# Products into unread columns at the heads of three attentions, and 128-row score products in the last attention, of a two-layer decoder

## The reference

```
x = x + L0_attn(ln(x))            # 16 gated heads, 4 causal heads, 4 meta heads, mixed
x = x + L0_xattn(ln(x), ctx)      # cross attention
x = x + L0_ffn(ln(x))             # 8 experts, 2 chosen, and 2 shared; GELU
x = x + L1_attn(ln(x))            # attention on fake-quantised (8 bit) q, k, v
x = x + L1_xattn(ln(x), ctx)      # cross attention, 16 heads of 8 dimensions
x = x + L1_ffn(ln(x))             # 16 experts, 2 chosen, and a shared one; SiLU
```

```
q = (x @ Wq + bq).reshape(B, N, 16, 8)
k = (y @ Wk + bk).reshape(B, M, 16, 8)
v = (y @ Wv + bv).reshape(B, M, 16, 8)
attn = softmax(einsum('bnhd,bmhd->bhnm', q, k) / sqrt(8))
out = einsum('bhnm,bmhd->bnhd', attn, v)
```

## Time and profile before

| what | value |
|---|---|
| median of 3 runs | 769.51 us (767.5 to 772.55) |
| profiled execution | 776.76 us |
| its span, first to last instruction | 775.0 us |
| PE busy | 638.4 us (82%) |
| DVE busy | 419.2 us (54%) |
| ACT busy | 374.7 us (48%) |
| POOL busy | 97.2 us (13%) |
| mean granted clock of PE over the span | 0.830 |

### The profile page before, as it was taken

One profiled execution on the slowest core, in us unless ns is written; L12 is line 12 of the kernel. 1 busy time (PEld: TensorE's weight loads), 2 busy tenths in 40 slices (PEclk: granted clock), 3 DMA queues, 4 the chain that ended last, 5 costly groups with the idle time before them and its releaser, 6 DMA issues. The chain is left out here.

```text
span 775.0 us, 9266 instructions
## 1 busy us (share of the span) xinstructions
PE 638.4 (82%) x3271; PEld 329.1 (42%) x3271; DVE 419.2 (54%) x824; ACT 374.7 (48%) x649; POOL 97.2 (13%) x78
## 2 busy tenths in 40 slices
PE   3389899899996965999999973888888389985798
PEld 1122223223343334898999941122221233333586
DVE  7377775776326645512222358878970754214555
ACT  2157776666650523554444512577876135533331
POOL 7211100100010002600000003960000000003000
PEclk9669999999995756799999966689995655557899
DMA  4342201550023054000000000000000020000000
GB/s 140 81 66 32 69 2 26 68 74 1 2 40 43 0 202 175 1 1 5 10 1 1 1 1 0 1 2 2 2 2 1 1 83 3 3 1 0 1 1 27
DMA packets 14017, 22.68 MB, mean 29 GB/s; under 512 B 2916, under 2 KB 9044, under 8 KB 13588
## 3 DMA queue, kind: packets, MB, share of 16 engines
q1 hardware_dynamic: 12436, 20.78, 11.7%
q10 hardware_dynamic: 1536, 1.31, 0.6%
HBM read 9.99 MB, written 0.52 MB: 14 GB/s over the span
## 5 line engine op out<-in xcount | busy, mean ns | idle before, releaser
L509 DVE TENSOR_REDUCE negmax<-ps 128x2 f32<-128x1024 f32 x96 | 113.8, 1216 | 37.9 <-PE ps L438 37.5
L556 ACT ACTIVATE probs<-ps 128x512 f32<-128x512 f32 x192 | 105.9, 596 | 41.5 <-PE ps L459 40.7
L556 ACT ACTIVATE probs_q<-ps,score_scale 128x512 f32<-128x512 f32 x128 | 78.2, 685 | 16.6 <-PE ps L459 15.5
L1671 PEld LDWEIGHTS ps<-wproj,hid 128*128 128x128 f32 x640 | 83.1, 191 | 6.5
L1671 PE MATMUL ps<-wproj,hid 128*128 128x128 f32 x640 | 83.8, 274 | 0.0
L1724 ACT ACTIVATE hid<-ps 128x512 f32<-128x512 f32 x80 | 47.6, 598 | 66.9 <-PE ps L818 66.9
L818 PE MATMUL ps<-h,wfc 128*128 128x512 f32 x240 | 76.5, 430 | 0.0
L509 DVE TENSOR_REDUCE negmax_q<-ps 128x2 f32<-128x1024 f32 x64 | 73.9, 1205 | 3.9 <-PE ps L438 3.9
L1832 DVE SCALAR_TENSOR_TENSOR x_tok<-ps,comb,x_tok 128x128 f32<-128x128 f32 x64 | 18.0, 344 | 69.6 <-PE ps L1671 69.6
L473 PE MATMUL ps<-probs_q,v_q 128*32 128x512 f32 x256 | 46.8, 730 | 0.0
L438 PE MATMUL ps<-k_gated,q_gated 64*128 64x512 bf16 x128 | 29.8, 427 | 20.1 <-DMA q_gated<-parts 9.3
(11 more groups left out here) (358 smaller groups left out, 931.9 us busy)
## 6 DMA issues: line engine op xcount, KB each, us to landing
q_wide<-parts SPq DMA_DIRECT2D x12, 256.0 KB, 5.7
k_wide<-parts SPq DMA_DIRECT2D x12, 256.0 KB, 7.1
wfc<-in_L_ffn_Wfc_dram SPq DMA_DIRECT2D x1, 2560.0 KB, 9.3
wproj<-in_L_ffn_Wproj_dram SPq DMA_DIRECT2D x1, 2560.0 KB, 15.1
k_gated<-parts SPq DMA_DIRECT2D x9, 128.0 KB, 2.4
q_gated<-parts SPq DMA_DIRECT2D x9, 128.0 KB, 2.4
w<-in_L_ffn_W_dram SPq DMA_DIRECT2D x1, 1024.0 KB, 17.0
square_weights<-in_squares_dram SPq DMA_DIRECT2D x1, 768.0 KB, 7.1
```

The costliest lines, as they stand in the source:

```text
L509: nc.vector.tensor_reduce(maxima, scores, AX.X, ALU.max, negate=True).then_inc(self.a_max_done, 1)
L556: nc.scalar.activation(self.probs[0:size, g % self.P_SLOTS, :], ps[0:size, self.B_BANK + g % self.B_SLOTS, :], ACT.Exp, scale=scale).then_ ...
L1671: last = nc.tensor.matmul(K.ps[:, y_bank(g), i * P:(i + 1) * P], hid[:, m % SLOTS, i * P:(i + 1) * P], wproj[:, FT * e + f, :], start=(f = ...
```

## The change

The change has four edits.

1. `CrossJob.q_at` and `k_at` give all 128 rows. A score product B of the last attention so multiplies all four heads' queries with the block-diagonal keys of one head. The zeros drop out, the result is the same.
2. `keep_busy(K, bank, count)` is new: count products of two weight tiles (128 rows, 128 x 128, float32) into the last 128 columns of a bank, where nothing reads them. `_keep_busy` puts such steps ("K") into the order ahead of every block A up to the first V: `first` of them ahead of the first A, into the given bank, and `each` ahead of the others, into bank 7. The three attentions have (16, 2), (12, 1) and (6, 2).
3. In the quantised attention `within=1` adds one such product to each of the 64 blocks A, behind its wait for the slot and into its own bank, before A writes over it.
4. Two waits for bank 7: the first attention waits for the second of DVE's gate sums, and the first job of the quantised attention for both halves of v scaled by ACT.

```diff
 class CrossJob
     def q_at(self, j, t0, n, more):
-        return self.q[32 * j:32 * j + 32, self.heads[0] // 4, t0:t0 + n]
+        return self.q[:, self.heads[0] // 4, t0:t0 + n]
     def k_at(self, j, t0, n, more):
-        return self.k[32 * j:32 * j + 32, self.heads[0] // 4, j, t0:t0 + n]
+        return self.k[:, self.heads[0] // 4, j, t0:t0 + n]
 class Attention
+    def _keep_busy(self, first, each, bank):
+        head = next(n for n, step in enumerate(self.order) if step[0] == "V")
+        order, count = [], first
+        for step in self.order[:head]:
+            if step[0] == "A":
+                order += [("K", count, bank)] if count else []
+                count, bank = each, self.O_BANK
+            order.append(step)
+        self.order = order + self.order[head:]
     def tensor(self, pe):
         for step in self.order:
             kind, u, i = step
+            if kind == "K":
+                keep_busy(K, i, u)
+                continue
...
                 self.slot_free(pe, step)
+                keep_busy(K, self.bank_of[step], self.within)
                 for half in range(2):
...
+def keep_busy(K, bank, count):
+    for _ in range(count):
+        K.nc.tensor.matmul(K.ps[:, bank, 3 * P:4 * P], K.squares[:, 0, :], K.squares[:, 1, :], start=True, stop=True,
+                           skip_group_check=True)
 GatedAttention
+                         busy=(16, 2, 7))
 gated_attention, tensor
             ln.wait_half(pe, 0)
+            pe.wait_ge(gate_sum, 2)
             att.tensor(pe)
 quantised_attention
-    jobs[0].after = [(n["first_strip"], 2), (n["q_scaled"], 2)]
+    jobs[0].after = [(n["first_strip"], 2), (n["q_scaled"], 2), (n["v_scaled"], 2)]
...
+                         busy=(12, 1, 1), within=1)
 cross_attention_heads
-    att = Attention(K, "attx", jobs, 4, 6, *attention_buffers(sb, "x", st))
+    att = Attention(K, "attx", jobs, 4, 6, *attention_buffers(sb, "x", st), busy=(6, 2, 7))
```

More of the change, by code:

```diff
@@ L278, with __init__ @@
     A_BANK, B_BANK, O_BANK = 0, 4, 7
-    def __init__(self, K, tag, jobs, lead, lead_blocks, probs, osb, negmax, prologue=(), extras=None, held=(), evacuate_on_vector=False):
-        self.evacuate_on_vector = evacuate_on_vector
+    def __init__(self, K, tag, jobs, lead, lead_blocks, probs, osb, negmax, prologue=(), extras=None, held=(), evacuate_on_vector=False,
+                 busy=(0, 0, 7), within=0):
+        self.evacuate_on_vector, self.within = evacuate_on_vector, within
         self.K, self.jobs, self.lead, self.lead_blocks = K, jobs, lead, lead_blocks
@@ L316, in __init__ @@
         self._schedule(extras or {}, held)
+        self._keep_busy(*busy)
         self.free_at, self.count, self.bank_of, uses = {}, {}, {}, []
@@ L893, in decoder_kernel @@
         modulation = sb("modulation", [16, D + 1])
+        K.squares = squares_sb
         for i, n in enumerate(SQUARES):
@@ L976, in __init__ @@
         self.bias_added = K.sem("bias_added")
-        super().__init__(K, "att0", jobs, lead, 8, *bufs[:3], prologue=prologue, extras=extras, held=held)
+        super().__init__(K, "att0", jobs, lead, 8, *bufs[:3], prologue=prologue, extras=extras, held=held,
+                         busy=(16, 2, 7))
         self.mixes = [s for s in self.order if s[0] in "CD"]
@@ L1996, in quantised_attention @@
         jobs[5 * b].after_v = [(n["v_ready"], b + 1)]
-    att = QuantAttention(K, "attq", jobs, 2, 8, *attention_buffers(sb, "q", st), evacuate_on_vector=True)
+    att = QuantAttention(K, "attq", jobs, 2, 8, *attention_buffers(sb, "q", st), evacuate_on_vector=True,
+                         busy=(12, 1, 1), within=1)
     def strip_of(ops, which, g, b):
```

## The result

| | before | changed |
|---|---|---|
| median | 768.81 us (7 runs, 767.5 to 772.55) | 760.58 us (7 runs, 756.01 to 766.0) |
| ratio | | 0.9891, 95% interval 0.9855 to 0.9928 |
| profiled execution, its span | 776.76, 775.0 us | 766.0, 764.2 us |
| PE busy, mean granted clock | 638.4 us, 0.830 | 651.2 us, 0.897 |

The account below looks back on a forecast made before the run. The last attention was taken as bound by PE at half clock. Gains of 17 (last), 1 (first), 0 (quantised head) and 1 (quantised middle) sum to 19 us: median 769.51 to 750.5 us, range 741 to 763.

Parts of the forecast that it names:

- Quantised attention, middle: Between its V: added products lose 3 us (0 to 14), clock returns 4; net 1 us gained, bounds 5 gained, 10 lost.
- the 4 us for the clock: Middle of the quantised attention: clock held at 1.00 instead of 0.92 gives back up to 5.5 us, 4 taken.
- Quantised head: Start of the quantised attention: first A 1.5 us late (1.1 to 2.3), 1.7 back by the first V; net 0.
- The tail: Quantised attention, V after the last A: no added products there, so it keeps its half clock.
- Last attention: B on 128 rows and added products raise the clock: group 7.44 to 4.6 us, 17 us gained, bounds 8 and 21.
- rows in use matter: PE in the last attention, saturated at half clock: rows in use, not busy time alone, seem to decide the clock.
- The price of B on 128 rows: Last attention: paired B run one behind the other, costing 0.21 us per group at full clock, 0.43 at half.
- First attention: Its 38 added products: 1.4 us lost on late blocks, 2.4 gained by earlier clock; net 1 gained, bounds 4 gained, 2 lost.
- The rival "slower": Quantised attention: products ahead of the 64 blocks A become its bound, at half clock 32 us over 26 pairs; 783 us, chance 0.05.

Follow-up runs that it names:

- the 32-column kernel: Changed kernel, with the product ahead of each of the 64 blocks A of the quantised attention cut from 128 to 32 columns; 791.66 us.

## Why the prediction was right or wrong, point by point

The forecast was 750.5 us and the measured time 760.58: sign right, inside the range given (741 to 763), size wrong by 10 us (8.2 gained where 19 were forecast). Of the terms:

- **The step that failed: "Quantised attention, middle".** It found "up to 3.0 us in the worst case" from V to V and 14 us over 26 pairs, and then: "most would fall into idle time; I take 3", less 4 for the clock, net 1 gained. Measured: 3.01 and 3.22 us where 2.48 us lay between two V, 14.03 against 12.14 us a period, and 10.4 us between the medians of the kernels with and without the 64 products. The worst case was right, and the choice inside 0 to 14 failed. By the shown windows PE is busy about 10.1 us of a period without the products (60.06 of 72) and 13.6 with them (82.82 of 85.3). So of 3.5 us of added PE time only 1.6 fell into idle time and 1.9 made the period longer. In the stretches shown, two products of 0.42 less the one wait of 0.30 make 0.54, and the distance grew by 0.53. The busy shares (69.3 of 82 us) couldn't tell this: the longer waits of PE, 1.00 ahead of T and 0.84 ahead of an A, stand in the other distances. The product was also priced by its time in a row of its like, 0.27 us; among 32-row products it holds PE 0.42 us, and the A that had begun beside a B waits for both. Of the 4 us for the clock little was the products' to give. The middle of the kernel before has four dips of 3.4 us, which made a distance 1.1 to 1.3 us longer each, but the same order has none in five other profiles and one in two.
- **Quantised head**: first A forecast 1.5 us late after the spread, measured 1.9 (1.7 in absolute time); the first V 1.3 late instead of level. The tail stayed at half clock in the profiled execution, as said.
- **Last attention**: mechanism right, size low. 4.33 us a group (4.6 forecast), the last groups 3.57, 3.1 twice and 2.36; 21.2 us instead of 17, and 20.9 as medians of the kernel with this part alone. The reason given, that rows in use matter, is half of it: B on 128 rows brings the clock up, but with the 24 products at the head B of 32 rows keep it up too. So the gain would have come by either edit, and the forecast didn't tell them apart.
- **The price of B on 128 rows** (0.21 us a group) didn't show: 4.33 with 128 rows, 4.43 with 32. By the speed-up that the Trainium skill gives for four 32-row products (TensorE: Matmul & The Clock Gate, Part 3, packing small matmuls) it was 7 us in all, an estimate; the trace disagrees for the last attention, where B of 32 rows mostly stood alone anyway. For the quantised one its rule agrees with the trace: products of different strips run at once, and what comes between them takes that away.
- **First attention**: 1 us gained was forecast with bounds of 4 and -2; the kernel with these products alone is 1.2 us faster, within an interval that holds zero.
- **The rival "slower"** had 0.05 with "at full clock 3.0 is the worst I find" against it. Its condition, the half clock, is what two experiments ran into (medians 792.8 and 791.7 us). Why it stayed out of the changed kernel wasn't argued, and the runs don't show it: in that the low chance was luck.

As shifts between the two profiled executions: +10.7 us at the first A of the last attention, -21.2 in that attention, -2.1 in the next products behind it (at full clock now), and +1.9 that a later block gives back. The sum is -10.7, and the two differ by 10.8 (776.76 to 766.0).

## What to carry to other kernels

An added instruction on an engine with idle time is free only as far as waits of that engine shrink by it: look for the waits row by row, between the place where it goes in and the next instruction that another engine waits for, and not at the busy share. Take the worst case where no such wait is found. On TensorE look also at what ran side by side there: a full product between two products of different row strips costs more than its columns. And when two edits lift the same clock, try each alone: here B on 128 rows without any added product gives 750.7 us, where all four edits gave 760.6.

## What was not expected of the hardware

- The granted clock depends on what went before: the same order of work in the last attention ran at 0.50 with PE busy 22.3 of 22.3 us and, after products of 128 rows at its head, at 1.00 with PE busy 12.93 of 13.3 (the kernel with the 24 products alone). The Trainium skill (same page, Part 1, the HAM clock gate) has sustained activity bring up the full clock; 59.6 of 59.6 us busy at 0.50 (the 64 products alone) show that a PE without a gap is not enough here.
- A 128x128 product between 32-row ones holds PE for 0.42 us, a second one right behind it only 0.23 more (0.65 for both), and one of 32 columns 0.34: about 0.2 us or more belong to the place and not to the columns.
- Small additions can leave the clock down for long: with one product between A and B, PE stood at half clock for 50 to 60 us in two kernels. With the same products in a row ahead of V, and no head products, its mean was 0.80 in the 17 us after the first V and 0.98 from 500 to 580 us. Why, no run here shows. Also open is why the 32-column kernel fell to half clock in all four executions in spite of its head products, and the 128-column one, by its mean clocks (0.897 to 0.914), in none of its seven.
